# Decoder layer with routed experts: a slot tile taken for eight steps at once, three tiles behind the last step, programs written out, two row tiles turned later

## The chip, the cores and the metric

One core of a Trainium2 chip (trn2) runs the whole kernel as one launch. The metric is device time in microseconds (us) of one execution; the time before is the median of three runs, 3820.38 us (3818.23 to 3829.71). The engines are TensorE (PE, matrix products), VectorE (DVE), ScalarE (ACT), GpSimd (POOL, here mostly gathers and scatters) and SyncE (SP, which issues the loads). Each runs its own program, and they meet at semaphores.

## The reference

A decoder layer on x (16 x 224 tokens, width 512): self-attention (16 heads of 64, with rotary positions), cross-attention to a context of 750 rows, and a mixture of experts. All three act on a layer-normed input and are added to x. The part that matters here:

```python
E, K, CF = 8, 2, 1.25               # N = 3584 tokens, F = 2048
capacity = int(CF * N / E)          # 560 slots per expert
probs = softmax(xf @ router_w.T); topw, topi = top_k(probs, K)
disp[e, pos] = xf[token]            # the tokens with the largest weights, up to 560
g = einsum('ecd,edf->ecf', disp, wg)
u = einsum('ecd,edf->ecf', disp, wu)
eo = einsum('ecf,efd->ecd', silu(g) * u, wd)
out[token] += eo[e, pos] * weight
```

## The kernel before

Each fp32 product is made of three fast ones (`mm3`, lines 26 to 31): both factors are split into a high half (a rounded copy, ACT) and a low half (the difference, DVE), and hi*hi, hi*lo and lo*hi are added up in PSUM. In the profile these are the lines L32, L33 and L34.

The last stage is `experts`. It first finds, per expert, the 560 tokens (a search with 15 small steps of DVE and PE), makes tables of their places (`table`, a matmul per token group, then `tables` on DVE), gathers their rows (POOL, `xg`) and turns them with PE transposes, five row tiles of 128, 128, 128, 128 and 48 slots (`turn_first` for expert 0, `turn` for the later ones). ACT and DVE split each turned tile into x_hi and x_lo (`split_x`).

Then come eight experts of FT = 16 steps. A step f covers 128 of the 2048 hidden columns. On PE it is two halves s of 280 slots (`up`): 12 matmuls of the gate product into psG (a unit), 12 of the up product into psU. ACT makes silu of psG (act_g), DVE multiplies it with psU (hid), ACT and DVE split hid into hid_hi and hid_lo and the next weights into halves (`high`, `low`). Between the halves and behind the second, PE does the down product of the step before (`down`): for slot tiles 0 to 3 three matmuls of 512 columns each into a PSUM bank psY of the tile's own. It waits for d_lo, the low half of the down weights. The fifth tile has 48 slots only and isn't split: it takes the unsplit raw_d and hid, in calls with 256 columns for each of the two sides of the output, and does so for two steps at a time (k = 0, 1), four calls, at every second step, ahead of tile 0:

```python
for k in range(2):
    for side in range(2):
        m = pe.matmul(psY[t][side * HALF_P:side * HALF_P + REST, 0:HALF_D], h[k][:, cols],
                      raw_d[k][:, side * HALF_D:(side + 1) * HALF_D], ...)
```

The profile shows two records for each of these calls (L2113, x8 for a group of four). At an expert's end the down product of step 15 follows for all five tiles; DVE adds each tile, times the token's weight, to the gathered output rows (`add_up`, L2430), and POOL scatters them (L2020).

The order of the work on every engine is the order in which it is written. Expert 0 is written out. Experts 1 to 6 are a loop of three turns with two experts each (`Fori(0, (E - 2) // 2)`), in which a part of the steps is an inner loop with two steps a turn; expert 7 stands behind it. PE, ACT and DVE all have these loops (L2161, L2234 and L2457 are the outer ones). The turning of the next expert's rows lies in steps 11 to 15. SP loads the weights of step f + 2 (gate, up) and of step f (down) in a loop of its own; raw_g, raw_u, raw_d and hid have two buffers each.

Of the kernel before, what the change touches and what calls it, by code (L numbers as in the profile page):

```python
# [1829 lines left out]
TABLE_AT = range(4, 4 + E - 2)  # L1830


def experts(nc, out, w_g, w_u, w_d, cst, rows_w, logits):

    with ExitStack() as c:
# [36 lines left out]
        raw_g, raw_u, raw_d = ([sb(f"raw_{m}{i}", [P, D]) for i in range(2)] for m in "gud")  # L1872
# [4 lines left out]
        act_g, h, h_hi, h_lo = ([sb(f"{n}{i}", [P, CAP], dt) for i in range(2)]  # L1877
# [23 lines left out]
        LOOPED = (TURN_AT - 1) // 2  # L1901
# [17 lines left out]
        with nc.Block() as block:  # L1919
            @block.sync  # L1920
            def _(sp):
# [14 lines left out]
                def fetch_down(e, f, i, first, half=None):  # L1936

                    cols = slice(f * P, f * P + P) if isinstance(f, int) else bass.ds(f * P, P)
                    if not first:
                        if i:  # L1940
                            hold(sp, S["gate"], S["up"], 4 * (FT * e + f) - 1)
# [3 lines left out]
                    sp.dma_start(raw_d[i][:], v).then_inc(load["d"][i], 16)  # L1945

                def fetch_expert(e, start, last):
                    with sp.Fori(start, FT // 2 - 1) as q:
                        for i in range(2):
                            fetch_up(e, 2 * q + 2 + i, i, False)  # L1950
                            fetch_down(e, 2 * q + i, i, False, q)
                    for i in range(2):
                        if not last:
                            fetch_up(e + 1, i, i, False)
                        fetch_down(e, FT - 2 + i, i, False)
# [3 lines left out]
                for i in range(2):  # L1959
                    fetch_up(0, i, i, True)  # L1960
                    fetch_down(0, i, i, True)
# [4 lines left out]
                fetch_expert(0, 1, False)  # L1966
# [64 lines left out]
            def _(pe):  # L2031
# [33 lines left out]
                def turn_first():  # L2065
                    for t in range(SLOT_TILES):
# [33 lines left out]
                def down(n, i, first, last, tiles, e=None, opens=True, begins=False):  # L2100
# [3 lines left out]
                    for t in tiles:  # L2104
# [15 lines left out]

                for i in range(2):
                    table(0, i)
                turn_first()

                def expert(e, j, last):
# [3 lines left out]
                    if start:  # L2129
                        pe.wait_ge(S["x_lo"], SLOT_TILES)  # L2130
                    up(n, 0, j, 1)

                    def step(m, i, f=None):
                        up(m, i, j, 0)
                        down(m - 1, 1 - i, f == 1, False, (0, 1) if i else (SLOT_TILES - 1, 0), None if start else e, True, f == 2)
                        if start and f in (2, 3):
                            table(1, f - 2)
                        elif start and f is not None and f - 1 in TABLE_AT:
                            table(f - 3, 0)
                        elif not last and f is not None and f >= TURN_AT:  # L2140
# [3 lines left out]
                        if start and f is not None and f - 1 in TABLE_AT:  # L2144
                            table(f - 3, 1)

                    if start:
                        for f in range(1, FT):
                            step(n + f, f % 2, f)
                    else:  # L2150
                        step(n + 1, 1, 1)
                        step(n + 2, 0, 2)
                        with pe.Fori(1, LOOPED) as q:
                            for i in (1, 0):
# [342 lines left out]
```

## Time and profile before

| | |
|---|---|
| median of three runs | 3820.38 us |
| profiled execution | 3824.65 us, span 3822.9 |
| PE busy | 3649.8 us (95%), 28214 matmuls |
| DVE, ACT, POOL busy | 2361.8, 1732.4, 1302.7 us |
| granted PE clock, mean | 0.978 |
| experts | from about 2547 us to the end |

The span is what the trace holds; the time of the same execution is 1.75 us more. The clock is the share of PE's full rate that was granted: 1.00 is 2.4 GHz, 0.50 is 1.2 GHz. PE is busy nearly all the time, so the questions are what its stream is made of and why it stands where it does.

### The profile page before, as it was taken

How to read it: one execution, taken by the hardware profiler on the slowest of the kernel's cores; microseconds unless marked ns; L12 is line 12 of the kernel's file. 1: busy time of each engine (PE TensorE's matmuls, PEld its weight loads, DVE VectorE, ACT ScalarE, POOL GpSimd, SP SyncE). 2: the span in 40 equal slices, each digit the busy share in tenths (PEclk: the TensorE clock that was granted, in tenths of full speed). 3: DMA queues.
4: the chain of work that ended last, by engine and by line, in shares of the span. 5: the costliest groups of instructions: out<-in, count | busy, mean ns of one | idle time of the engine just before them, and what ended most of it. 6: DMA issues, size and time to landing. Idle time of an engine off the chain costs nothing. (4 is left out here: it accounts for less than half of the span.)

```text
span 3822.9 us, 85100 instructions
## 1 busy us (share of the span) xinstructions
PE 3649.8 (95%) x28214; PEld 3133.9 (82%) x28214; DVE 2361.8 (62%) x5547; ACT 1732.4 (45%) x4277; POOL 1302.7 (34%) x1385
## 2 busy tenths in 40 slices
PE   7999999999979999999999999759999999999999
PEld 6888888888768888888888888548889898888988
DVE  6788888888846666666666666566443334334343
ACT  4555555454535555555555555313333333333332
POOL 1333333333325555665556666310101101011010
PEclk9999999999989999999999999769999999999999
DMA  4222122222243434444343443223423323233232
GB/s 123 60 55 62 53 62 53 63 54 63 78 122 93 110 103 106 115 109 116 98 111 104 107 116 87 78 58 89 121 78 121 117 81 118 85 112 120 81 106 67
DMA packets 315021, 349.28 MB, mean 91 GB/s; under 512 B 45308, under 2 KB 232036, under 8 KB 314884
## 3 DMA queue, kind: packets, MB, share of 16 engines
q1 hardware_dynamic: 305796, 318.26, 30.4%
q0 software_dynamic: 9088, 29.17, 2.4%
q8 instruction: 89, 1.46, 0.2%
q14 instruction: 48, 0.39, 0.0%
HBM read 183.23 MB, written 38.91 MB: 58 GB/s over the span
## 5 line engine op out<-in xcount | busy, mean ns | idle before, releaser
L1605 DVE TENSOR_REDUCE x_mx<-x_psS 112x1 f32<-112x752 f32 x512 | 479.7, 937 | 387.0 <-PE x_psS L1158 383.0
L2396 DVE TENSOR_TENSOR hid<-e_psU,act_g 128x280 f32<-128x280 f32 x256 | 115.1, 450 | 670.6 <-PE e_psU L34 670.6
L1440 ACT ACTIVATE x_pt<-x_psE 125x448 f32<-125x448 f32 x768 | 389.5, 542 | 229.8 <-PE x_psE L1170 220.4
L1029 POOL TENSOR_TENSOR part<-x_pt 125x448 f32<-125x448 f32 x255 | 292.4, 1147 | 511.1 <-ACT x_pt L1440 502.1
L2020 POOL DMA_INDIRECT out<-ex_y,sidx x40 | 41.4, 1034 | 1042.0 <-DVE ex_y L2430 1034.3
L611 POOL TENSOR_TENSOR qks<-qks,cos 128x448 f32<-128x448 f32 x128 | 147.7, 1154 | 679.6 <-DMA qks<-qk 679.6
L2176 ACT ACTIVATE act_g<-e_psG 128x280 f32<-128x280 f32 x256 | 103.7, 405 | 466.4 <-PE e_psG L34 465.5
L32 PE MATMUL e_psG<-ex_hi,g_hi 128*128 128x280 f32 x1024 | 303.8, 297 | 9.6 <-issue 9.6
L1158 PE MATMUL x_psS<-k_st,q_st 97*112 97x376 f32 x1024 | 287.3, 362 | 23.1 <-DMA k_st<-mk 14.9
L32 PE MATMUL pj<-xT_hi,win_hi 128*128 128x224 f32 x1024 | 302.9, 296 | 1.4 <-DVE xT_lo L651 1.3
L34 PE MATMUL e_psG<-ex_hi,g_lo 128*128 128x280 f32 x1024 | 299.2, 292 | 0.0
L1031 POOL TENSOR_TENSOR part<-part,x_pt 125x448 f32<-125x448 f32 x255 | 292.3, 1146 | 20.0
L32 PE MATMUL e_psU<-ex_hi,u_hi 128*128 128x280 f32 x1024 | 298.8, 292 | 0.0
L33 PE MATMUL e_psG<-ex_lo,g_hi 128*128 128x280 f32 x1024 | 298.7, 292 | 0.0
L34 PE MATMUL e_psU<-ex_hi,u_lo 128*128 128x280 f32 x1024 | 298.4, 291 | 0.0
L33 PE MATMUL e_psU<-ex_lo,u_hi 128*128 128x280 f32 x1024 | 297.8, 291 | 0.0
L34 PE MATMUL pj<-xT_hi,win_lo 128*128 128x224 f32 x1024 | 282.3, 276 | 0.0
L33 PE MATMUL pj<-xT_lo,win_hi 128*128 128x224 f32 x1024 | 281.7, 275 | 0.0
L1170 PE MATMUL x_psE<-q_st,k_st 99*125 99x224 f32 x1536 | 262.7, 280 | 6.4 <-ACT x_pt L1440 4.1
L1170 PEld LDWEIGHTS x_psE<-q_st,k_st 99*125 99x125 f32 x1536 | 235.8, 190 | 15.6 <-ACT x_pt L1440 10.7
L2180 ACT ACTIVATE hid_hi<-hid 128x280 fp32r<-128x280 f32 (+1 forms) x256 | 107.2, 419 | 287.5 <-DVE hid L2396 287.5
L674 DVE CUSTOM_DVE_ANT_0 pr<-psS,mask 112x112 f32<-112x112 f32 (+1 forms) x512 | 139.4, 328 | 130.5 <-issue 69.6
(299 smaller groups left out, 10887.6 us busy)
## 6 DMA issues: line engine op xcount, KB each, us to landing
k_st<-kT SPq DMA_DIRECT2D x768, 93.8 KB, 2.2
raw_g<-in_L_ffn_wg SPq DMA_DIRECT2D x128, 256.0 KB, 2.9
raw_u<-in_L_ffn_wu SPq DMA_DIRECT2D x128, 256.0 KB, 2.8
raw_d<-in_L_ffn_wd SPq DMA_DIRECT2D x128, 256.0 KB, 2.8
qks<-qk SPq DMA_DIRECT2D x512, 56.0 KB, 2.0
q_st<-qT SPq DMA_DIRECT2D x384, 56.0 KB, 2.0
ctxt<-in_ctx SPq DMA_DIRECT2D x16, 1125.0 KB
xt<-in_x SPq DMA_DIRECT2D x16, 448.0 KB, 3.7
```

The costliest lines, as they stand in the source:

```text
L32: pe.matmul(out, lh, rh, start=first, stop=False)
L33: pe.matmul(out, lh, rl, start=False, stop=False)
L34: return pe.matmul(out, ll, rh, start=False, stop=last)
L611: pool.tensor_tensor(qks[i][:], qks[i][:], cos[:].unsqueeze(1).to_broadcast((P, 2, T)), ALU.mult)
L674: m = dve.tensor_tensor_reduce(pr[par][:, hd, to:to + n], psS[hd][0:HT, to:to + n], mask[:, h, 0:n], -SD ** -0.5, -NEG, ALU.add, ALU.min, ...
L1029: pool.tensor_tensor(part[:], pt[j][:, 0, :], pt[j][:, 1, :], ALU.add).then_inc(parted, 1)
L1031: pool.tensor_tensor(part[:], part[:], pt[j][:, 2, :], ALU.add).then_inc(parted, 1)
L1158: m = pe.matmul(psS[0:HT, s, 0:376], q_st[0:97, head, h * HT:(h + 1) * HT], k_st[4 * (g % 2) + j][0:97, SHALF[s]], start=True, stop=True)
L1170: m = pe.matmul(psE[(j + i) % 2][0:KR, s * T:(s + 1) * T], k_st[4 * (g % 2) + j][0:99, r * KR:(r + 1) * KR], q_st[0:99, 4 * g + j, :], sta ...
L1440: act.activation(pt[j][:, i, :], psE[(j + i) % 2][0:KR, 0:2 * T], ACT.Exp, scale=XD ** -0.5).then_inc(exp_done, 1)
L1605: dve.tensor_reduce(mx[:, j, h:h + 1], psS[0:HT, :, 0:376], AX.XY, ALU.max).then_inc(s_taken, 1)
L2396: dve.tensor_tensor(h[i][:, halves[s]], psU[:, 0:CH], act_g[i][:, halves[s]], ALU.mult).then_inc(S["mul"], 1)
```

## The change

- **Fifth slot tile.** RING = 8: raw_d and hid get eight buffers. The fifth tile is done for eight steps in one group of 16 calls, at step 8 (for steps 0 to 7) and at the expert's end (for 8 to 15). SP's waits for the down loads are rewritten for it.
- **Tiles behind the last step.** At step 15 only slot tile 0 stands between the halves; 1, 2 and 3 are behind the second.
- **Programs written out.** PE has no loops in this stage; ACT, DVE and SP have no inner loops any more, and keep the outer one.
- **Opening.** PE gets filler matmuls (`keep_awake`, 12, 12 and 3 x 2, into psU, whose content is overwritten); row tiles 3 and 4 of expert 0 are turned behind the first half of step 0 and not ahead of it.

```diff
+RING = FT // 2
-        raw_g, raw_u, raw_d = ([sb(f"raw_{m}{i}", [P, D]) for i in range(2)] for m in "gud")
+        raw_g, raw_u, raw_d = ([sb(f"raw_{m}{i}", [P, D]) for i in range(RING if m == "d" else 2)] for m in "gud")
-        act_g, h, h_hi, h_lo = ([sb(f"{n}{i}", [P, CAP], dt) for i in range(2)]
+        act_g, h, h_hi, h_lo = ([sb(f"{n}{i}", [P, CAP], dt) for i in range(RING if n == "hid" else 2)]
...
-                def fetch_down(e, f, i, first, half=None):
+                def fetch_down(e, f):
+
+                    cols = slice(f * P, f * P + P)
+                    if f >= 2 or not below(e, 1):
+                        hold(sp, S["gate"], S["d_hi"], FT * e + f - 1)
+                    if f >= RING:
+                        hold(sp, S["gate"], S["d_used"], (FT - 1) * e + f - RING + 1)
+                    elif not below(e, 1):
+                        if f < RING - 1:
+                            hold(sp, S["gate"], S["d_used"], (FT - 1) * e + f - RING + 2)
                         else:
-                            hold(sp, S["gate"], S["d_used"], FT // 2 * e + (f // 2 if isinstance(f, int) else half))
+                            hold(sp, S["gate"], S["y_full"], SLOT_TILES * e)
...
+                def keep_awake(n):
+
+                    for _ in range(n):
+                        pe.matmul(psU[:], same[:], g_hi[0][:], start=True, stop=True)
+
-                def turn_first():
-                    for t in range(SLOT_TILES):
+                def turn_first(tiles):
+                    for t in tiles:
...
-                            for k in range(2):
+                            for k in range(RING):
                                 for side in range(2):
                                     m = pe.matmul(psY[t][side * HALF_P:side * HALF_P + REST, 0:HALF_D], h[k][:, cols],
                                                   raw_d[k][:, side * HALF_D:(side + 1) * HALF_D], start=begins and k == 0,
-                                                  stop=last and k == 1)
-                                if k == 0:
+                                                  stop=last and k == RING - 1)
+                                if not (last and k == RING - 1):
                                     m.then_inc(S["d_used"], 1)
...
+                first_half = range((SLOT_TILES + 1) // 2)
+                pe.wait_ge(S["gu_hi"], 1)
+                keep_awake(12)
                 for i in range(2):
                     table(0, i)
-                turn_first()
+                keep_awake(12)
+                for t in first_half:
+                    turn_first([t])
+                    keep_awake(2)
...
                     up(n, 0, j, 0, start)
                     if start:
+                        turn_first(range(len(first_half), SLOT_TILES))
                         pe.wait_ge(S["x_lo"], SLOT_TILES)
                     up(n, 0, j, 1)
 
-                    def step(m, i, f=None):
+                    def step(m, i, f):
+                        near = (SLOT_TILES - 1, 0) if f == RING else (0,) if f == FT - 1 else (0, 1)
                         up(m, i, j, 0)
-                        down(m - 1, 1 - i, f == 1, False, (0, 1) if i else (SLOT_TILES - 1, 0), None if start else e, True, f == 2)
+                        down(m - 1, 1 - i, f == 1, False, near, None if start else e, True, f == RING)
...
-                        down(m - 1, 1 - i, f == 1, False, (2, 3) if i else (1, 2, 3), None, False)
+                        down(m - 1, 1 - i, f == 1, False, range(near[-1] + 1, SLOT_TILES - 1), None, False)
...
-                expert(0, 0, False)
-                with pe.Fori(0, (E - 2) // 2) as r:
-                    for i in range(2):
-                        expert(2 * r + 1 + i, 1 - i, False)
-                expert(E - 1, 1, True)
+                for e in range(E):
+                    expert(e, e % 2, e == E - 1)
...
                 def expert(e, j, last):
-                    n, half = FT * e, FT // 2 * e
-                    step(n, half, 0)
-                    with act.Fori(0, LOOPED) as q:
-                        step(n + 2 * q + 1, half + q, 1)
-                        step(n + 2 * q + 2, half + q + 1, 0)
-                    for f in range(2 * LOOPED + 1, FT):
+                    for f in range(FT):
                         turned = None if last or f < TURN_AT else (e + 1, 1 - j, f - TURN_AT)
```

Order on PE, expert 0, before: the first group of the fifth tile, in step 2, between the first half's up unit (psU) and tile 0. Rows are line, operation, output<-inputs and output shape.

```order
L34 MATMUL e_psU<-ex_hi,u_lo 128x280
L2113 MATMUL e_psY<-raw_d,hid 48x256 x4
L32 MATMUL e_psY<-d_hi,hid_hi 128x512
L33 MATMUL e_psY<-d_lo,hid_hi 128x512
L34 MATMUL e_psY<-d_hi,hid_lo 128x512
```

And of the change, the first group of expert 0, in step 8:

```order
L34 MATMUL e_psU<-ex_hi,u_lo 128x280
L2125 MATMUL e_psY<-raw_d,hid 48x256 x16
L32 MATMUL e_psY<-d_hi,hid_hi 128x512
L33 MATMUL e_psY<-d_lo,hid_hi 128x512
L34 MATMUL e_psY<-d_hi,hid_lo 128x512
```

The place within a step is the same; there are 2 groups of 16 calls in an expert and not 8 of 4.

Order on PE in the opening, before, from the turning of the places (g_pos) to the first gate unit (psG):

```order
L2048 MATMUL e_psY<-r_ident,g_pos 112x128 x2
L2055 MATMUL e_psY<-value,onelo 128x10 x32
L2062 MATMUL e_psT<-r_ident,xg 128x128 x4
L2062 MATMUL e_psY<-r_ident,xg 128x128 x16
L32 MATMUL e_psG<-ex_hi,g_hi 128x280
```

And of the change (L2075 are the fillers, L2069 the turning of the rows):

```order
L2055 MATMUL e_psY<-r_ident,g_pos 112x128 x2
L2075 MATMUL e_psU<-g_hi,r_same 128x512 x12
L2062 MATMUL e_psY<-value,onelo 128x10 x32
L2075 MATMUL e_psU<-g_hi,r_same 128x512 x12
L2069 MATMUL e_psT<-r_ident,xg 128x128 x4
L2075 MATMUL e_psU<-g_hi,r_same 128x512 x2
L2069 MATMUL e_psY<-r_ident,xg 128x128 x4
...
L32 MATMUL e_psG<-ex_hi,g_hi 128x280
...
L34 MATMUL e_psU<-ex_hi,u_lo 128x280
L2069 MATMUL e_psY<-r_ident,xg 128x128 x8
L32 MATMUL e_psG<-ex_hi,g_hi 128x280
```

The last two row tiles (x8) now stand behind the 24 matmuls of the first half.

Order on ACT, the head of the outer loop, before: one step of expert 1, then the inner loop begins.

```order
L2234 UNCONDITIONAL_BRANCH
L2234 ISA
L2176 ACTIVATE act_g<-e_psG 128x280
...
L2180 ACTIVATE hid_hi<-hid 128x232
L2170 ACTIVATE d_hi<-raw_d 128x512
L2213 UNCONDITIONAL_BRANCH
L2213 ISA
```

And of the change:

```order
L2239 UNCONDITIONAL_BRANCH
L2239 ISA
L2186 ACTIVATE act_g<-e_psG 128x280
...
L2190 ACTIVATE hid_hi<-hid 128x232
L2178 ACTIVATE d_hi<-raw_d 128x512
L2185 ISA
L2186 ACTIVATE act_g<-e_psG 128x280
```

The inner loop is gone, the steps follow each other. From the outer loop's first branch to the one that closes it, the order has 225 rows on ACT before and 399 after; on DVE 269 and 487.

## Rows read from the trace of the kernel before

**Rows 1.** stretches of PE work: us, busy (records) per engine, clock, DMA share, GB/s

```profile
2550.00:2705.00 155.00, 155.00 (x1230) 139.26 (x1229) 93.57 (x159) 52.65 (x114) 9.04 (x7) 1.00 0.30 88
3181.00:3337.00 156.00, 155.18 (x1045) 140.10 (x1045) 61.85 (x123) 54.25 (x119) 16.30 (x17) 1.00 0.36 105
```

**Rows 2.** PE in time, one group: start us, us, engine, line, operation, shapes, count

```profile
2904.10 0.29 PE L34 MATMUL e_psU<-ex_hi,u_lo 128*128 128x280 f32 x1
2904.32 1.07 PE L2113 MATMUL e_psY<-raw_d,hid 128*48 128x256 f32 x8
2904.57 0.82 PE L2113 MATMUL e_psY<-raw_d,hid 128*48 128x256 f32 x6
2904.78 0.60 PE L2113 MATMUL e_psY<-raw_d,hid 128*48 128x256 f32 x4
2905.32 0.51 PE L32 MATMUL e_psY<-d_hi,hid_hi 128*128 128x512 f32 x1
2905.66 0.40 PE L33 MATMUL e_psY<-d_lo,hid_hi 128*128 128x512 f32 x1
2905.89 0.40 PE L34 MATMUL e_psY<-d_hi,hid_lo 128*128 128x512 f32 x1
```

**Rows 3.** the end: PE and POOL in time

```profile
3810.30 0.50 PE L32 MATMUL e_psY<-d_hi,hid_hi 128*128 128x512 f32 x1 [0.90 <-DVE d_lo L2243]
3813.18 1.02 POOL L2020 DMA_INDIRECT out<-ex_y,sidx  x1 [137.30 <-DVE ex_y L2430]
3818.81 0.99 POOL L2020 DMA_INDIRECT out<-ex_y,sidx  x1 [0.30 <-issue]
```

**Rows 4.** DMA issues of the page: queue, count, KB each, us to landing

```profile
raw_d<-in_L_ffn_wd SPq DMA_DIRECT2D x128, 256.0 KB, 2.8
```

**Rows 5.** PE in time, first tile of the last down product, four experts

```profile
3018.87 0.51 PE L32 MATMUL e_psY<-d_hi,hid_hi 128*128 128x512 f32 x1 [0.83 <-DVE d_lo L2243]
3182.51 0.50 PE L32 MATMUL e_psY<-d_hi,hid_hi 128*128 128x512 f32 x1 [0.82 <-DVE d_lo L2243]
3338.47 0.50 PE L32 MATMUL e_psY<-d_hi,hid_hi 128*128 128x512 f32 x1 [0.82 <-DVE d_lo L2243]
3500.54 0.51 PE L32 MATMUL e_psY<-d_hi,hid_hi 128*128 128x512 f32 x1 [0.83 <-DVE d_lo L2243]
```

**Rows 6.** PE in time and the stretch behind, at the outer loop's turn

```profile
3028.06 0.57 PE L32 MATMUL e_psG<-ex_hi,g_hi 128*128 128x280 f32 x1 [5.13 <-issue]
3028.00:3033.60 5.60, 5.54 (x24) 5.57 (x25) 0.00 (x0) 0.92 (x2) 2.03 (x3) 0.50 0.16 41
```

**Rows 7.** sequencer of DVE (L2457), ACT (L2234), 3022 to 3031: ns min/median/max, starts

```profile
L2457 DVEq COMPARE_BRANCH  x1: 56/56/56, 3023.2 to 3023.2; - x1
L2457 DVEq FUSED_REGOPS  x1: 118/118/118, 3027.0 to 3027.0; - x1
L2234 ACTq COMPARE_BRANCH  x1: 45/45/45, 3023.9 to 3023.9; - x1
L2234 ACTq FUSED_REGOPS  x1: 89/89/89, 3024.1 to 3024.1; - x1
```

**Rows 8.** stretch ahead of expert 0

```profile
2534.50:2546.70 12.20, 5.23 (x20) 3.63 (x21) 7.32 (x22) 2.39 (x4) 8.44 (x9) 0.50 0.45 124
```

**Rows 9.** PE in time, first turned row tile, second half of step 0

```profile
2539.62 1.11 PE L2062 MATMUL e_psT<-r_ident,xg 128*128 128x128 f32 x4 [5.30 <-DMA xg<-expert_rows,gather_rows]
2550.88 0.29 PE L32 MATMUL e_psG<-ex_hi,g_hi 128*128 128x280 f32 x1
```

**Rows 10.** ACT and DVE in time, opening of expert 0

```profile
2545.61 0.60 ACT L2197 ACTIVATE ex_hi<-e_psY 128x512 fp32r<-128x512 f32 x1 [0.83 <-PE e_psY L2062]
2549.52 0.41 ACT L2176 ACTIVATE act_g<-e_psG 128x280 f32<-128x280 f32 x1 [2.00 <-PE e_psG L34]
2547.73 1.56 DVE L2341 TENSOR_TENSOR value<-onehi,r_consts 112x560 bf16<-112x560 f32 x2
```

**Rows 11.** DMA queues in the stretch 2550 to 2705

```profile
q8 instruction: 9, 0.15, 0.4%
```

More of the change, by code:

```diff
@@ L1965, in _ @@
                     fetch_up(0, 2 + i, i, False)
-                fetch_expert(0, 1, False)
+                for f in range(2, FT):
+                    if f + 2 < FT:
+                        fetch_up(0, f + 2, f % 2, False)
+                    else:
+                        fetch_up(1, f + 2 - FT, f % 2, False)
+                    fetch_down(0, f)
                 with sp.Fori(1, E - 1) as e:
@@ L2144, in step @@
-                        if start and f is not None and f - 1 in TABLE_AT:
+                        down(m - 1, 1 - i, f == 1, False, range(near[-1] + 1, SLOT_TILES - 1), None, False)
+                        if start and f - 1 in TABLE_AT:
                             table(f - 3, 1)
[L2147 to L2154, printed above, removed]
-                                step(n + 2 * q + 2 - i, i)
-                        for f in range(2 * LOOPED + 1, FT):
-                            step(n + f, f % 2, f)
@@ L2168, in high, with step @@
                 def high(m, i, value, raw, hi, count):
-                    act.wait_ge(load[m][i], value)
-                    act.activation(hi[i][:], raw[i][:], ACT.Copy).then_inc(S[count], 1)
-                def step(n, half, i, next_=True, turned=None):
+                    act.wait_ge(load[m][i % 2], value)
+                    act.activation(hi[i % 2][:], raw[i][:], ACT.Copy).then_inc(S[count], 1)
+                def step(n, e, f, next_=True, turned=None):
+                    i, half = f % 2, FT // 2 * e + f // 2
                     def silu(s):
@@ L2192, in step @@
                     split_h(1)
[L2193 removed]
+                    high("d", f % RING, 16 * (half + 1), raw_d, d_hi, "d_hi")
                 def split_x(e, i, t, bank=psT):
@@ L2210, in expert @@
                 def expert(e, j, last):
-                    n, half = FT * e, FT // 2 * e
-                    step(n, half, 0)
-                    with act.Fori(0, LOOPED) as q:
-                        step(n + 2 * q + 1, half + q, 1)
-                        step(n + 2 * q + 2, half + q + 1, 0)
-                    for f in range(2 * LOOPED + 1, FT):
+                    for f in range(FT):
                         turned = None if last or f < TURN_AT else (e + 1, 1 - j, f - TURN_AT)
-                        step(n + f, half + f // 2, f % 2, not last or f + 1 < FT, turned)
+                        step(FT * e + f, e, f, not last or f + 1 < FT, turned)
                     if not last:
@@ L2434, in expert @@
                     n = FT * e
-                    step_of(n, 0)
-                    with dve.Fori(0, LOOPED) as q:
-                        step_of(n + 2 * q + 1, 1)
-                        step_of(n + 2 * q + 2, 0)
-                    for f in range(2 * LOOPED + 1, FT):
+                    for f in range(FT):
                         turned = None if last or f < TURN_AT else (e + 1, 1 - j, f - TURN_AT)
-                        step_of(n + f, f % 2, not last or f + 1 < FT, None, turned)
+                        step_of(n + f, f % 2, f % RING, not last or f + 1 < FT, None, turned)
                     add_up(e)
```

44 lines of the change are left out of this document (19 added, 25 removed).

## The prediction, made before the change was run

> **What bounds the kernel now.** I read the stretches first. From 2550 us on the program is eight experts one behind the other, and TensorE (PE) is busy 155.18 of 156.00 us at clock 1.00 in one of them [rows 1]. VectorE (DVE) is busy 61.85 us there, ScalarE (ACT) 54.25. So a microsecond counts only if it is taken from PE's own stream or from one of the few places where PE stands. Some experts are longer than that for the same matmuls; [rows 5] show them.
>
> **Part 1, the fifth slot tile for eight steps at once.** PE's order in time shows what a group of the 48-row tile costs [rows 2]. The last up matmul before it starts at 2904.10, the first full tile behind it starts at 2905.32, and only the next one, at 2905.66, begins a run at the normal pace. From 2904.10 to 2905.66 is 1.56 us. Two normal steps belong to others: 0.13 us for an up matmul and 0.23 for a down one (2905.66 to 2905.89). A group so costs 1.20 us. Its eight records start in pairs 0.215 us apart (2904.57, 2904.78), which makes 0.86 us of matmuls and **0.34 us for going in and coming out**. A group of 16 calls instead of 4 has 16 pairs: 16 x 0.215 + 0.34 = 3.78 us. An expert has eight groups now and two after, so it goes from 9.60 to 7.56, by 2.04 us. In seven experts that is 14.3 us.
>
> In the last expert the last group is in the tail. POOL's scatters start at 3813.18 and the fifth starts at 3818.81, each behind the one before [rows 3], while the group's five tiles began at 3810.30. After the change the fifth tile ends some 2.6 us later relative to that start, near 3817, its add near 3817.6, and the fifth scatter, 1.0 us behind an add as the first one is, could go at about 3818.6: still in its slot. So on the path are seven groups before (8.4 us) and one after (3.8): 4.6 us. Part 1 is worth **18.9 us**. Bounds: were the pairs 0.23 us apart (the mean of the merged row: 1.07 less a duration of 0.38, over three intervals), 16.3 us would be left; nothing in the rows lets it be more than 20. The buffers that now hold eight steps cost no wait: the load for step 8 is released when PE has read the first slot, near the start of the group in step 8, and ACT wants it at that step's end, some 8 us later by the pace of [rows 2], against 2.8 us to landing [rows 4].
>
> **Part 2, three tiles behind the last step.** At an expert's end PE waits for the low half of the last down weights; the wait is there each time, 0.82 or 0.83 us, at 3018.87 as at 3338.47 [rows 5]. With what the stopped weight load adds it is near 1.0 us from start to start. The chain is multiply, split, high half, low half, and it begins when the last up unit ends. Two tiles cover it now. A third, three matmuls of 0.23 us, covers 0.70 us more. So 8 x 0.70 = **5.6 us**; zero if the chain moved with it, 7.9 if the whole wait went. It can't move: the tile is taken from the gap between the two halves of the step, where the multiply of the first half is done about 0.9 us after its unit and is wanted not before 2.2 us.
>
> **Part 3, the programs written out.** Last wait to last wait is 163.64 us in one expert, 155.96 in the next, 162.07 in the one behind [rows 5]. The two long ones each hold a turn of the outer loop: PE stands 5.13 us with no releaser, then runs its first 24 matmuls at clock 0.50 [rows 6]. The stands and the slow clock behind them are 7.68 + 6.11 = 13.8 us, and PE has no branch any more.
>
> But ACT and DVE keep their outer loop, and its body grows because the inner loop is gone. What a far branch costs is seen on DVE: COMPARE_BRANCH at 3023.2, next instruction at 3027.0, **3.7 us**; on ACT the same pair is at 3023.9 and 3024.1 [rows 7]. DVE's body has 269 rows in the order of the program, ACT's 225. After the change they have 487 and 399, so ACT's is above the length that stopped DVE, and I take 3.7 us for ACT too. Who waits for it: PE would start the new expert at about 3022.9, finish the first gate and up units 24 x 0.13 us later, and then wants ACT's silu of the first. ACT's branch is at 3023.9, ACT is back at 3027.6, its silu starts near 3027.9 and takes 0.41 [rows 10]: PE waits from 3026.0 to 3028.4, 2.4 us, twice. DVE is back at 3027.0, before that silu has ended, so its stand is hidden behind ACT's. Part 3 is 13.8 - 4.9 = **8.9 us**. Bounds: 13.8 if ACT doesn't stand, and 3.9 if the two waits also bring the slow clock of [rows 6], at most 2.5 us each.
>
> The Trainium skill, "Runtime: NRT & Kernel Launch", section "Instruction fetch mechanics", says that a taken branch to a target outside the current two pages has to fetch it, and that engines other than TensorE hold 512 instructions. By that length ACT's 399 would fit and part 3 would be 13.8; that is rival A. The trace speaks against the length, as DVE stood with 269 rows.
>
> **Part 4, the opening.** Before expert 0 the clock is 0.50 [rows 8]. The change puts 12 + 12 filler matmuls of 512 columns around the table matmuls and two behind each of three row tiles. At the slow clock one should take twice 0.23, so 12 take 5.6 us: the first dozen runs from 2526.5 to about 2532 and delays the first table half, which nobody needs before the second, at 2533.7; the second dozen ends before 2540, while the rows' arrival lets the first turn go at 2539.62 [rows 9]. They are hidden; if the second dozen stays slow it costs up to 0.3.
>
> Two row tiles move behind the first half. The third tile's low half is ready near 2545.1 to 2545.6, so the first unit starts there instead of behind all five turns. With the full clock it ends, with its up unit, near 2548.2. Then come the two turns, and now ACT's splits, wcol and silu and DVE's splits stand between them and the second half: 0.60 us for the fourth tile's high half, half as much for the short fifth's, 0.41 for silu [rows 10] and wcol, with the turn's own 0.6 some 2.2 us in all. So the second half starts at about 2550.7, and started at 2550.88 [rows 9]. Behind the splits DVE still has 1.56 us of table values before the first multiply [rows 10], which makes the second up unit wait 0.4. So with the full clock it is 0.2 lost; with the clock still at 0.50 for the first dozen matmuls 2.2 lost, up to 2.5. I take **-0.8**, with +0.3 as the good end. What was won by starting early is given back as a wait for the late tiles.
>
> **Sum.** 18.9 + 5.6 + 8.9 - 0.8 = 32.6 us. The profiled execution took 3824.65 us (span 3822.9), so 3792.1 for one like it; the median of the three runs is 4.3 us under it, so **3788 us**, 0.85% less than before. A measurement here tells about 0.3%, 11.5 us, from nothing.
>
> **Rivals.**
> A. ACT doesn't stand at its branch. For it: ACT stood 0.2 us so far. Against: DVE at 269 rows. Then 4.9 us more, 3783. Chance 0.15.
> B. The gains of parts 1 and 2 hold, but the waits for ACT bring the slow clock and the opening stays slow: 5.0 + 1.7 less, and with the upper bound of the pairs 2.6 less again, 3795 to 3797. For it: a stand of 5.13 us left the clock at 0.50 [rows 6], and the new ones are half as long. Against: the stands of 0.82 us leave the stretch at 1.00 [rows 1, 5]. Chance 0.22.
> C. Slower: the written-out PE program has to be fetched. Expert 0 is written out already, and in 155 us its instruction queue moves 9 packets in 0.4% of 16 engines' time, 1.1 us each [rows 11]. Seven experts would fetch 63. If PE stood the whole 1.1 us at each, 69 us, the time would be 3857; from 0.5 us each the change is slower. Against it: PE is busy 155.00 of 155.00 us in expert 0 [rows 1]. Chance 0.03.
> D. The change doesn't do what it says: the group pays per pair and not per group, so that 16 calls cost four times 1.20. Then part 1 gives only the tail's 3.6, and the time is 3803. Against: the pairs inside a group are evenly spaced and the long steps are at its edges [rows 2]. Chance 0.04.
>
> **Chances and range.** My forecast keeps 0.56. Faster by over 0.3% holds in the forecast, A, B and D: 0.96; within 0.3% 0.02 (C with fetches mostly hidden), slower 0.02. The range takes in A with its good opening (3782) and B with its bounds (3797): 3780 to 3798.
>
> **What would show it.** In the profile after: 16 groups of 32 records, each about 3.8 us from edge to edge; PE's wait for the low half at an expert's end near 0.2 us; seven experts of about 153.3 us and two places, after experts 2 and 4, where PE waits some 2.4 us for ACT's silu and ACT's COMPARE_BRANCH is followed by 3.7 us of nothing; a PE wait of 1 to 2 us between the halves of the first step. PE gaps without a releaser inside experts 1 to 7 would make it wrong on C; experts near 155 us would make part 1 wrong.

## The result, and the profile after

The changed kernel takes 3788.13 us (median of 4 runs, 3781.80 to 3793.32) against 3820.24 us for the kernel before on the same chip (median of 4, 3818.23 to 3829.71). The ratio is 0.9916, with a 95% interval of 0.9903 to 0.9929. The forecast was 3788 us. Its profiled execution took 3791.84 us with a span of 3790.1, which is 32.8 us less than the one that the prediction was made against.

The page of the changed kernel, one line per engine and then the two instruction queues (packets, MB, share of 16 engines):

```profile
PE 3640.3 (96%) x28244; PEld 3139.0 (83%) x28244; DVE 2363.4 (62%) x5547; ACT 1730.3 (46%) x4277; POOL 1299.5 (34%) x1385
q8 instruction: 106, 1.74, 0.2%
q14 instruction: 67, 0.55, 0.0%
```

These shares say little, as PE is busy nearly all the time before and after. The kernel has to be read by places. The best ruler is the start of the first tile of an expert's last down product, the instruction of [rows 5]. A distance below is the time from one such start to the next. A turn is a distance in which an outer loop branches back, in the kernel before or in this one. In the kernel before these starts are 155.97 us apart, and 163.64 and 162.07 us where the outer loops turn. In the changed kernel they are 153.29 apart, and 155.00 at the two turns. Two such stretches side by side, from first tile to first tile (us, busy time and records per engine, clock, DMA share, GB/s):

```profile
2856.44:3009.73 153.29, 153.17 (x1044) 140.50 (x1044) 61.83 (x122) 54.22 (x118) 16.17 (x17) 1.00 0.35 107
3009.73:3164.73 155.00, 153.73 (x1044) 140.60 (x1044) 61.82 (x122) 54.10 (x118) 16.30 (x17) 1.00 0.35 106
```

PE is busy 153.17 of 153.29 us in the first. In the second it stands some 1.3 us, and the clock stays at 1.00. The stretch of the kernel before that answers to the second one was 163.64 us long.

The group of the fifth tile, PE in time (the columns of [rows 2]):

```profile
2624.98 0.29 PE L33 MATMUL e_psU<-ex_lo,u_hi 128*128 128x280 f32 x1
2625.10 0.29 PE L34 MATMUL e_psU<-ex_hi,u_lo 128*128 128x280 f32 x1
2625.32 3.66 PE L2125 MATMUL e_psY<-raw_d,hid 128*48 128x256 f32 x32
2628.91 0.50 PE L32 MATMUL e_psY<-d_hi,hid_hi 128*128 128x512 f32 x1
2629.25 0.39 PE L33 MATMUL e_psY<-d_lo,hid_hi 128*128 128x512 f32 x1
2629.48 0.40 PE L34 MATMUL e_psY<-d_hi,hid_lo 128*128 128x512 f32 x1
```

From 2625.10 to 2629.25 is 4.14 us by the unrounded starts. Less the two ordinary steps, 0.13 and 0.23, a group of 32 records takes 3.78 us. It comes twice in an expert, where groups of 1.20 us came eight times.

The same tile as in [rows 5], at the turn of the loops and one expert on:

```profile
3317.52 0.40 PE L34 MATMUL e_psY<-d_hi,hid_lo 128*128 128x512 f32 x1
3318.03 0.51 PE L32 MATMUL e_psY<-d_hi,hid_hi 128*128 128x512 f32 x1
3318.38 0.39 PE L33 MATMUL e_psY<-d_lo,hid_hi 128*128 128x512 f32 x1
```

From 3317.52 to 3318.03 is 0.51 us. In the kernel before the same step, from start to start, was 1.22. The waits from 2700 us on, all that PE has left (total us, times, longest):

```profile
PE e_psG L32 <- ACT act_g L2186: 2.0, 2, 1.2
PE e_psY L32 <- DVE d_lo L2248: 0.4, 2, 0.2
PE e_psU L32 <- DVE hid L2401: 0.3, 1, 0.3
```

So the low half of the down weights has gone from eight waits of 0.82 us to 0.2 us, and the new waits at the turns are there: one for ACT's silu at each, and a shorter one for DVE's multiply. This is where they come from, PE, ACT and DVE in time at the first turn:

```profile
3019.38 0.29 PE L34 MATMUL e_psU<-ex_hi,u_lo 128*128 128x280 f32 x1
3020.82 0.40 PE L32 MATMUL e_psG<-ex_hi,g_hi 128*128 128x280 f32 x1 [1.15 <-ACT act_g L2186]
3017.23 0.21 ACT L2218 ACTIVATE wcol<-xg 128x5 f32 x1 [8.27 <-DVE ex_y L2435]
3020.36 0.40 ACT L2186 ACTIVATE act_g<-e_psG 128x280 f32<-128x280 f32 x1 [2.92 <-PE e_psU L34]
3022.13 0.45 DVE L2401 TENSOR_TENSOR hid<-e_psU,act_g 128x280 f32<-128x280 f32 x1 [5.11 <-issue]
```

and the sequencers' own rows there, ACT first, then DVE (duration ns, first and last start):

```profile
L2239 ACTq COMPARE_BRANCH  x1: 45/45/45, 3017.3 to 3017.3; - x1
L2239 ACTq FUSED_REGOPS  x1: 84/84/84, 3020.2 to 3020.2; - x1
L2458 DVEq COMPARE_BRANCH  x1: 74/74/74, 3016.6 to 3016.6; - x1
L2458 DVEq FUSED_REGOPS  x1: 110/110/110, 3019.7 to 3019.7; - x1
```

ACT stands 2.9 us behind its branch, where it had stood 0.2 [rows 7], and its silu is the first thing behind that. DVE stands 3.0 us, where it had stood 3.7.

The opening, PE in time, from the fillers to the second half of step 0; [rows 9] answer to the third and the last row:

```profile
2529.77 1.68 PE L2075 MATMUL e_psU<-g_hi,r_same 128*128 128x512 f32 x6
2535.06 5.40 PE L2075 MATMUL e_psU<-g_hi,r_same 128*128 128x512 f32 x12
2540.50 0.66 PE L2069 MATMUL e_psT<-r_ident,xg 128*128 128x128 f32 x4
2546.34 0.40 PE L32 MATMUL e_psG<-ex_hi,g_hi 128*128 128x280 f32 x1 [0.94 <-DVE ex_lo L2394]
2549.55 1.04 PE L2069 MATMUL e_psY<-r_ident,xg 128*128 128x128 f32 x8
2551.83 0.40 PE L32 MATMUL e_psG<-ex_hi,g_hi 128*128 128x280 f32 x1 [1.24 <-DVE ex_lo L2394]
```

The first half now starts before the last two row tiles are turned, and PE then waits 1.24 us for the low half of the fifth one. The clock is 0.50 while the second dozen fillers runs and 1.00 from 2540.2 on, so the 24 matmuls of the first half run at full speed (0.13 us apart).

The end is POOL's, as before; the first and the last scatter:

```profile
3780.35 1.02 POOL L2027 DMA_INDIRECT out<-ex_y,sidx  x1 [135.92 <-DVE ex_y L2435]
3785.98 0.98 POOL L2027 DMA_INDIRECT out<-ex_y,sidx  x1 [0.30 <-issue]
```

The first is 2.88 us behind the start of tile 0, as in [rows 3], and the last is 5.63 us behind the first, also as there.

**The sum, by these landmarks.** Ahead of the experts the profiled execution is 0.87 us later for stages that the change leaves alone. From PE's transpose of the places (`g_pos`, 2525.86 and 2526.73) to the first matmul of step 1 it takes 28.70 us for 28.10. From step 1 to the first of the tiles it takes 147.72 for 152.97. The seven distances between the tiles together are 29.06 us shorter. From the last to the end it is 12.58 for 12.56. That makes +0.87 + 0.60 - 5.25 - 29.06 + 0.02 = -32.8 us. By parts, the turns give 13.8 - 3.4 = 10.4 (3.4 is what 155.00 has over 153.30, twice). The eight waits give 9.91 - 4.24 = 5.7, summed from start to start. What is left of the 34.3 us from step 1 to the last tile is 18.2. It holds the gain of the groups and whatever else changed; the groups alone are measured below.

### The profile page after: what moved, and what is told of

It reads as the page before. It is cut to its first block and busy times, and to the rows that moved or that the text cites. A ratio compares the mean times of both kernels' runs of the same rounds, so it can differ in the third digit from the quotient of the medians.

```text
span 3790.1 us, 84211 instructions
## 1 busy us (share of the span) xinstructions
PE 3640.3 (96%) x28244; PEld 3139.0 (83%) x28244; DVE 2363.4 (62%) x5547; ACT 1730.3 (46%) x4277; POOL 1299.5 (34%) x1385
```

## The experiments

All are edits of the changed kernel. A kernel that ran once is compared by its profiled distances between the tiles, and not by its total, which varies by 10 us. The distances repeat well, but not everywhere. In the first profile of the changed kernel, and in five edits that leave its groups and tiles alone (PE's loop, ACT out, ACT and DVE out, no fillers, turns ahead), every ordinary distance is 153.3 us within 0.1. A turn varies by some tenths.

Four kernels ran together, on another chip than the other edits: the full array, four tiles behind, the best version, and the changed kernel once more. In this second profile the changed kernel's distances were 153.94, 153.29, 155.55, 153.31, 155.66, 153.48 and 151.95, together 2.9 us more than in its first profile. The row that differs is ACT's first silu of an expert. Away from the turns it starts 1.85 us behind the first matmul of its gate unit in the first profile, and 2.05 to 3.45 us behind it in the second, with ACT idle. The distances are longer where it is later than 2.62 us.

### Groups of two and of four steps

```diff
-                        near = (SLOT_TILES - 1, 0) if f == RING else ...
+                        near = (SLOT_TILES - 1, 0) if f % GROUP == 0 else ...
...
-                            for k in range(RING):
+                            for k in range(k0, k0 + GROUP):
```

Buffers and written-out programs stay. With GROUP = 2 there are eight groups again, with GROUP = 4 four.

> The changed kernel with all its buffers and its written-out programs, but the fifth tile again in groups of two steps, 8 per expert. My theory, a fixed 0.34 us per group: an expert of the changed kernel (153.3 us from last wait to last wait) becomes 155.3, a group 1.20 us, and the whole 3784 to 3788 becomes about 18.8 us more, near 3805. Rival, the gain came from the straight program or from the buffers and not from the grouping: the expert stays at 153.3 and the time near 3788.

> Groups of four steps, 4 per expert. Fixed cost per group: a group is 8 x 0.216 + 0.34 = 2.07 us, the expert 153.3 + 2 x 0.34 = 154.0. Rival, the cost grows with the run of these calls or falls only at a threshold: the expert is at 153.3 or at 155.3 and not between.

Two steps: 3805.75 us (median of 5 runs, 3803.00 to 3811.54), ratio 0.9967 (0.9952 to 0.9982); the ratio of the changed kernel was 0.9916. One group of it, PE in time:

```profile
2621.59 0.29 PE L34 MATMUL e_psU<-ex_hi,u_lo 128*128 128x280 f32 x1
2621.81 1.07 PE L2126 MATMUL e_psY<-raw_d,hid 128*48 128x256 f32 x8
2622.81 0.51 PE L32 MATMUL e_psY<-d_hi,hid_hi 128*128 128x512 f32 x1
2623.15 0.39 PE L33 MATMUL e_psY<-d_lo,hid_hi 128*128 128x512 f32 x1
```

2621.59 to 2623.15 is 1.56 us, 1.20 net: the same as in [rows 2], so neither the deeper buffers nor the straight program changed the price of a group. The tiles are 155.43 us apart, 2.14 more than with groups of eight. Four steps: 3792.23 us in its one run, a group 2.42 us from edge to edge and 2.05 net, the tiles 154.00 apart. Net prices of 1.20, 2.05 and 3.78 for 4, 8 and 16 pairs lie on one line: 0.215 for a pair and 0.34 for a group. Rival D, by which four times as many pairs cost four times 1.20, falls; part 1 has the mechanism that the prediction gave it. From groups of two steps to groups of eight, the stretch from step 1 to the first tile is 4.7 us shorter and the seven distances together are 14.8 us shorter. So the groups are worth 19.5 us, measured directly. That is 1.3 more than the 18.2 left over above, so something else in the change costs 1.3 us; it isn't placed.

### What the 0.34 us is

```diff
-                                for side in range(2):
-                                    m = pe.matmul(psY[t][side * HALF_P:side * HALF_P + REST, 0:HALF_D], h[k][:, cols],
-                                                  raw_d[k][:, side * HALF_D:(side + 1) * HALF_D], ...
+                                m = pe.matmul(psY[t][:], h[k][:, CAP - P:CAP], raw_d[k][:], ...
```

> What makes the 0.34 us at a group's edges. In place of two calls of 48 weight columns and 256 data columns per step, one plain call of 128 weight columns (the last 128 slots) and 512 data columns, still unsplit fp32; the fifth tile's result is another one. Theory 1, the part-array tile needs it: with full-array calls the edges are gone, the step from the last up matmul into the group and from the group into tile 0 is that of the streams themselves, and only the group's inside is longer (8 calls of about 0.85 us). Theory 2, fp32 beside the split products needs it: the edges stay, some 0.1 going in and 0.2 coming out.

This kernel doesn't compute the layer's fifth tile; only its time is of use. 3844.83 us, one run. PE in time around its first group:

```profile
2628.25 0.29 PE L34 MATMUL e_psU<-ex_hi,u_lo 128*128 128x280 f32 x1
2628.38 7.03 PE L2124 MATMUL e_psY<-raw_d,hid 128*128 128x512 f32 x16
2634.84 0.80 PE L32 MATMUL e_psY<-d_hi,hid_hi 128*128 128x512 f32 x1
2635.48 0.40 PE L33 MATMUL e_psY<-d_lo,hid_hi 128*128 128x512 f32 x1
2635.72 0.39 PE L34 MATMUL e_psY<-d_hi,hid_lo 128*128 128x512 f32 x1
```

Going in takes an ordinary 0.13 us (2628.25 to 2628.38), where it takes 0.22 ahead of a 48-row group (2625.10 to 2625.32). From edge to edge it is 7.23 us; less 0.13 and 0.23 for the neighbours, 6.87 us are left for 16 records that start 0.429 us apart, 6.86. Nothing is left over. So the fixed 0.34 us does not come from the type of the operands, which is the same here. It goes with the form of the 48-row calls. That form differs in three things: a call uses a part of the array, it has 256 data columns and not 512, and the two sides' records start side by side (two records every 0.215 us). No run separates the three. The Trainium skill, "TensorEngine Tiling (Array Packing)", section "Key Properties", says that "Changing tiling mode (not just tile) drains the TensorE". These two groups agree with it; if that is the cause, 0.34 us is the price of one change in and out here.

### Two tiles and four behind the last step

```diff
-                        near = ... else (0,) if f == FT - 1 else (0, 1)
+                        near = ... else (0, 1)
```

The other kernel has () for (0,), so that no tile stands between the halves of the last step and all four stand behind it.

> The changed kernel with two tiles behind the last step again. My theory, the low half's chain counts from the last up unit: PE's wait before an expert's last down product is 1.22 us from start to start again (0.51 now), the expert 154.0 for 153.3, the whole 5.6 us more. Rival, the chain is bound by something earlier (the load or ACT's work of the first half): the wait stays nearer to 0.51.

> The changed kernel with all four full tiles behind the last step, none between its halves. My theory, each tile moved is 0.70 us of cover until the wait is used up: 0.51 us from start to start becomes the normal 0.23, an expert 153.0 for 153.3, the whole 2.2 us less. Rival, with nothing between the halves PE waits for the first half's multiply before the second up unit: the period stays at 153.3 or rises, with a PE wait there.

Two behind: the wait is back at each end of an expert,

```profile
PE e_psY L32 <- DVE d_lo L2248: 6.7, 8, 0.9
```

and the tiles are 153.99 apart, 0.70 more than with three; 3803.15 us in one run, whose opening was slow too (below). Four behind: the step to the tile is an ordinary 0.23 us in all eight experts, and three of the seven distances are 152.93, as expected 0.36 less. The other four are longer than that saving allows, by 0.3 to 0.8 us (153.60 behind expert 1, where PE's first matmul of the second half's gate unit starts 0.68 us behind the one before it). PE waits for ACT's silu at each of them, and away from the turns it is the late silu that the second profile of the changed kernel has too. The seven distances together are so only 0.5 us shorter than in the changed kernel's first profile, where 2.2 us were expected for the whole, but 3.3 us shorter than in its second one, on the same chip. 3794.82 us, one run, on a chip where the kernel before took 3828.27. The mechanism of part 2 is shown on both sides, at the wait itself: three matmuls more in front of it take three matmuls' time from it, until it is gone. What the fourth tile saves in the total isn't settled.

### PE's outer loop put back

```diff
-                for e in range(E):
-                    expert(e, e % 2, e == E - 1)
+                expert(0, 0, False)
+                with pe.Fori(0, (E - 2) // 2) as r:
+                    for i in range(2):
+                        expert(2 * r + 1 + i, 1 - i, False)
+                expert(E - 1, 1, True)
```

> The changed kernel with PE's outer loop restored, three turns of two experts, the steps inside written out. My theory, a far branch costs PE its stand of about 5 us and the slow clock behind it: the two experts behind a turn take 160 to 161.5 us and not 155.0, the whole is 10 to 13 us more, near 3799, and PE no longer waits for ACT's silu there. Rival, the stand came from the inner loops or from the registers and not from the branch of the outer loop: 155.0 stays.

3792.42 us (median of 4, 3789.46 to 3795.25), ratio 0.9922 (0.9905 to 0.9938), which its total alone doesn't tell from the changed kernel. The distances do: 159.17 and 157.94 at the turns, where I had expected 160 to 161.5 and a whole near 3799. PE at the turn, and the stretch from there:

```profile
3015.77 0.57 PE L32 MATMUL e_psG<-ex_hi,g_hi 128*128 128x280 f32 x1 [3.11 <-issue]
3016.14 0.43 PE L33 MATMUL e_psG<-ex_lo,g_hi 128*128 128x280 f32 x1
3014.90:3021.80 6.90, 6.03 (x26) 6.06 (x27) 0.06 (x1) 0.92 (x2) 3.15 (x5) 0.51 0.25 78
```

PE stands 3.1 us and not 5.13 [rows 6] (from start to start 3.49 and 3.44 at the two turns, before 5.51 and 4.89), and the slow clock follows it all the same. The obvious reading is that the longer group of the fifth tile, 32 records ahead of the branch instead of 8, covers more of the stand. The rows of PE's sequencer speak against it. The first two are of this kernel, the others of the kernel before (ns, start):

```profile
L2172 PEldq COMPARE_BRANCH  x1: 4916/4916/4916, 3010.4 to 3010.4; - x1
L2172 PEldq FUSED_REGOPS  x1: 77/77/77, 3015.4 to 3015.4; - x1
L2161 PEldq COMPARE_BRANCH  x1: 3347/3347/3347, 3019.6 to 3019.6; - x1
L2161 PEldq FUSED_REGOPS  x1: 73/73/73, 3023.0 to 3023.0; - x1
L2090 PEldq FUSED_REGOPS  x1: 46/46/46, 3027.8 to 3027.8; - x1
```

In both kernels the sequencer is at the branch while the group's matmuls are still to end: 2.2 us ahead of their end here (3012.66), and 3.4 us in the kernel before (3022.93). So the long group covers less of the stand, not more. What this kernel lacks is a second piece. Before, 4.8 us pass between the branch's register row and the next row (4.0 at the other turn); here it is 0.06. This kernel differs from the one before in the group and in PE's inner loops, which are written out, and no run tells which of them took the second piece away.

The turns so cost 10.5 us over two ordinary experts, against 3.4 in the changed kernel and 13.8 in the one before. Of part 3's 10.4 us, 7.1 come from writing out PE's outer loop. The other 3.3 are the difference between these two kernels with that loop, and their cause is open.

### ACT's outer loop written out, then DVE's too

```diff
-                with act.Fori(0, (E - 2) // 2) as r:
-                    for i in range(2):
-                        expert(2 * r + 1 + i, 1 - i, False)
+                for e in range(1, E - 1):
+                    expert(e, e % 2, False)
```

The second kernel has the same edit on DVE as well.

> The changed kernel with ACT's outer loop written out too; DVE keeps its own. My theory, of the two it is ACT's stand that PE waits for: both experts behind a turn take 153.3 us and not 155.0, 3.4 us in all, though DVE's branch is still followed by some 3 us. Rival, DVE's stand takes its place: 154 to 155 stays at those two experts, with a wait for DVE's hid before the second up unit.

> ACT's and DVE's outer loops both written out. All seven periods 153.3 (151.1 in the last), 3.4 us less than the changed kernel, near 3785 beside a changed kernel of 3788. If the longer programs had a cost of their own (more pages to fetch), the plain experts would be above 153.3.

ACT alone: 3788.54 us, one run, and the turns are 154.78 and 154.67, not 153.3: the rival of the expectation came out. The wait has moved by one unit, to DVE's multiply:

```profile
3019.68 0.40 PE L32 MATMUL e_psU<-ex_hi,u_hi 128*128 128x280 f32 x1 [1.19 <-DVE hid L2400]
3013.82 0.48 DVE L2434 SCALAR_TENSOR_TENSOR ex_y<-e_psY,wcol,ex_cur 128x256 f32<-128x256 f32 x1 [2.85 <-PE e_psY L2125]
3019.17 0.45 DVE L2400 TENSOR_TENSOR hid<-e_psU,act_g 128x280 f32<-128x280 f32 x1 [4.87 <-PE e_psG L34]
```

DVE's branch ends at 3014.00 and its next row is at 3016.84; a second register row ends at 3017.05, and then there is nothing until the multiply at 3019.17, although the matmuls that it reads had ended near 3017 and ACT's silu before. So DVE stands twice, 2.84 us and 2.1 us (2.74 and 2.15 at the other turn). That is what made "hidden behind ACT's" wrong. Both out: six distances are 153.37, the last 151.13, and the turns are gone. Its time was 3790.97 us, one run, where 3785 was expected; its opening took 31.5 us (below), 2.8 more than the changed kernel's. The three kernels together show that the 3.4 us left at the turns belong to ACT's and DVE's branches, each nearly covering the other. The two together gave 3.4 back, less 0.4 that the six distances lose by 0.07 each. ACT's alone gave 0.55, which is hardly more than what the turns vary by: with both loops kept they cost 3.1 and 3.3 us in the two kernels of the next section, and 4.6 with groups of four.

ACT's body had 399 rows and stood 2.9 and 2.6 us; with 225 rows it stood 0.2. The Trainium skill, "Runtime: NRT & Kernel Launch", section "Instruction fetch mechanics", gives these engines room for 512 instructions in blocks of 256, and says that a taken branch stalls when its target isn't in the current two pages. That a longer body stands agrees with it. But a body of 399 rows, or DVE's of 269, would fit into two pages, and both stood: to be shorter than 512 isn't enough here, and where the two pages lie at the branch no trace shows.

### The opening without fillers, and with all five tiles turned ahead

```diff
-                keep_awake(12)
                 for i in range(2):
                     table(0, i)
-                keep_awake(12)
                 for t in first_half:
                     turn_first([t])
-                    keep_awake(2)
```

The other kernel keeps the fillers and turns all five row tiles ahead of the first half, as the kernel before did.

> The changed kernel without the filler matmuls, the late turning kept. From the turning of the places to the first matmul of step 1 the changed kernel takes 28.7 us. My theory, the fillers buy the full clock for the first half and the late tiles cost the rest: without them the first 24 matmuls start at clock 0.50 and the stretch is 30.5 to 32 us. Rival, the clock would have risen by itself in time: 28.7 stays.

> The changed kernel with its fillers, but all five row tiles turned ahead of the first half, as before the change. My theory, turning two tiles late gives nothing: the wait between the halves (1.5 us for the splits, 0.4 for the table values) goes and the first unit starts about 0.9 us later, so the stretch is 26.5 to 27.5 us, for 28.7. Rival, the late turning is what hides the arrival of the last rows: then the first unit starts 2 us later and the stretch is 29 or more.

The measure is the stretch of above, from the transpose of the places to step 1. It is 28.10 us in the kernel before and 28.70 in the changed one. Without fillers it is 31.5 (3787.99 us, one run), and the slow transposes show why, in the first row the first tile's and in the second those of the two late tiles (four took 0.66 us at clock 1.00 in the changed kernel), between the halves:

```profile
2534.08 1.12 PE L2069 MATMUL e_psT<-r_ident,xg 128*128 128x128 f32 x4 [5.27 <-DMA xg<-expert_rows,gather_rows]
2545.88 1.15 PE L2069 MATMUL e_psY<-r_ident,xg 128*128 128x128 f32 x8
```

With the fillers and all turns ahead it is 26.90 (3785.76 us, one run), with no wait between the halves. So the fillers were worth 2.8 us in that pair, and turning two tiles later cost 1.8: between the halves, the late tiles' splits stand on DVE ahead of PE. But the fillers don't hold the clock each time. The changed kernel's opening took 28.7 to 29.1 us in five profiles (the changed one twice, groups of four, PE's loop, ACT out) and 30.2 to 31.5 in five others (groups of two, two behind, four behind, ACT and DVE out, full array), where the clock fell to 0.50 once more just ahead of or in the first half. Nothing in those edits touches the opening's order. What decides it from run to run is not settled. Over the ten the mean is 29.9 us, and the kernel without fillers ran once: so 2.8 us is what the fillers give when the clock holds, and what they give on average isn't shown. With all turns ahead the clock held in both profiles that there are, this one and the best version's.

### The best version, beside the changed kernel

ACT and DVE written out, four tiles behind, all five tiles turned ahead.

> The changed kernel with ACT's and DVE's outer loops written out, four tiles behind the last step and all row tiles turned ahead with the fillers kept: 3.4 + 2.2 + 1.8 us less than the changed kernel beside it, ratio to the kernel before near 0.9895; all periods 153.0.

> The changed kernel itself, as the measure for the run beside it: near 3788, ratio to the kernel before 0.991 to 0.992, periods 153.3 and twice 155.0. The stretch from the turning of the places to step 1 is 28.7 us if the clock stays at 1.00 behind the fillers and 30.8 to 31.5 if it falls once more.

It takes 3781.59 us (median of 4, 3775.10 to 3784.57), ratio to the kernel before 0.9871 (0.9853 to 0.9889). The changed kernel beside it takes 3789.38 us (median of 6, 3784.46 to 3796.42), ratio 0.9900 (0.9885 to 0.9915). The two medians are 7.8 us apart, where 7.4 was expected, and the intervals overlap by 0.0004, so it is very likely ahead, by some 0.2%. In the trace the opening is 26.73 us for 28.92. The expectation of 153.0 for every distance failed: three are 152.93, and the other four are 0.7 us longer than that, at the late silu of above:

```profile
3012.51 0.21 ACT L2218 ACTIVATE wcol<-xg 128x5 f32<-128x5 f32 x1 [8.58 <-issue]
3014.86 0.40 ACT L2186 ACTIVATE act_g<-e_psG 128x280 f32<-128x280 f32 x1 [2.14 <-PE e_psG L34]
```

The gate unit started at 3011.53 there, and the silu 3.33 us behind it; in an expert without the gap it is 2.58 us behind. ACT has nothing to do meanwhile, and no row and no instruction transfer on its queue stands beside it. The changed kernel's second profile has it at three of the five distances away from the turns, so it isn't an effect of the fourth tile or of the loops written out; the expectation of 153.3 and twice 155.0 for that profile failed by it. None of the nine profiles of changed kernels that were taken elsewhere has it away from the turns. The cause is open.

## Why the prediction was right, point by point

The time was right to 0.1 us, and that closeness is luck: the runs spread over 11.5 us, and the stages ahead of the experts, the same in every kernel here, ended anywhere from 2517.0 to 2530.7 us in the fourteen profiles. What matters is the sum by its terms, 18.9 + 5.6 + 8.9 - 0.8 = 32.6 forecast against 18.2 + 5.7 + 10.4 - 0.6 = 33.7 measured, with 0.9 us lost ahead of it to stages that the change doesn't touch.

**Part 1** held in its mechanism and size: a group of 16 calls was forecast at 3.78 us and took 3.78. Splitting eight records into pairs and edges was the step that did it, and groups of two and four steps confirmed both numbers. The 18.2 is only what is left when the other parts are taken out. Measured directly, groups of eight steps against groups of two, part 1 is 19.5 us, 0.6 above the forecast. The other 1.3 us, a cost that the prediction doesn't have, isn't placed. The tail behaved as described: the first scatter 2.88 us and the last 8.51 us behind tile 0, both as before. The load for step 8 cost nothing; PE has no wait on it.

**Part 2** held: 0.70 forecast at each wait, 0.71 measured, with 0.2 us of wait left. The point that the chain doesn't move with the tile was tested on both sides, by two tiles and by four.

**Part 3** had the right mechanism and two wrong prices. "I take 3.7 us for ACT too" was 2.9 and 2.6. "PE waits from 3026.0 to 3028.4, 2.4 us, twice" was 1.7 each in all. "Its stand is hidden behind ACT's" failed: DVE's comes in two pieces, and when ACT's branch was taken away 1.5 and 1.4 of the 1.7 us remained, as a wait for DVE. The forecast of 8.9 was so 1.5 too low. It also took the 13.8 us of the old turns as the price of PE's outer loop; in the changed kernel that loop costs 7.1 us, as the kernel with PE's loop shows. The other 3.3 went with the second piece of PE's stand, for a reason that no run shows.

**Part 4** came out near, -0.6 for -0.8. Forecast were a second half that starts little earlier or later than before, some wait for the late tiles, and 0.4 for the second up unit; measured, from the same landmark on, it starts 0.08 us later, after a wait of 1.24, with a step of 0.44 before the second up unit. What the prediction missed is that its two clock cases aren't the change's to choose: 28.7 and 30.2 to 31.5 us both occur, as often as each other, and the profile that it is held against is of the good kind. With the mean of the ten profiles, 29.9, part 4 would be -1.8. It also missed that the late turning itself costs: with the same fillers and all turns ahead the stretch is 26.9 us.

**Rivals.** A fell: ACT stands. B fell at the turns, where the clock is 1.00 in the stretch shown; but its other half, a slow opening, occurs in some executions. C fell: PE has no gap without a releaser in experts 1 to 7, while its queue moved 106 packets for 89. D fell to the groups of two and of four.

## What to carry to other kernels

When small calls come in groups, take the step from the last record before to the second one behind, subtract the ordinary steps, and split the rest into a price per call and a price per group: 0.34 us of each 1.20 was the group's, and fewer, longer groups saved it. When one engine's loop is written out, look at the branches of the engines that feed it as well, and count their stand up to the first real operation; two stands that hide each other must go together. A wait at the end of a chain shrinks by the independent work that is moved behind the chain's start, here 0.70 us for three matmuls, until it is gone. And profile the unedited kernel again beside each round of edits, before a difference of some tenths in one distance is put down to an edit.

## What the runs showed of the hardware

- A group of the 48-row matmuls between full-array ones costs 0.34 us beyond its 0.215 us per pair, with 4, 8 and 16 pairs alike; a full-array group of the same operand type costs nothing at its edges, but 0.429 us for each of its records.
- A far branch on DVE has a second stand: 2.84 us to the first register row, and 2.1 us more before the first vector operation, though its inputs were there (ACT's loop written out). With ACT's loop kept, the pieces were 3.0, 1.0 and 1.3 us between the rows.
- ACT stood 2.9 and 2.6 us at its far branch with a body of 399 rows, and 0.2 with one of 225.
- PE's sequencer was at the far branch 2.2 to 3.4 us before the matmuls ahead of it had ended. PE then stood 5.1 us in the kernel before, where its sequencer's stand has two pieces of 3.3 and 4.8 us, and 3.1 us in the changed kernel with PE's outer loop, where it has one of 4.9. In both cases the clock went to 0.50. Stands of 1.2 us left it at 1.00.
- The same fillers were followed by full clock in five profiles and by another fall to 0.50 in five others.
- ACT's first silu of an expert started 1.85 us behind the first matmul of its gate unit in the changed kernel's first profile, and 2.05 to 3.45 us behind it in the second, with ACT idle.
